# One-hots of four tiles: one comparison and one multiplication of 512 columns in place of four weighed comparisons of 128

## The chip, the cores and the metric

The kernel runs on one core of one Trainium2 chip. The metric is the device time of one launch in microseconds, the median of three runs. All data are fp32 unless said otherwise.

## The reference

A graph network of two layers over N = 6250 nodes with 96 features and E = 100000 edges, sorted by their target node `dst`, each with a source `src`, 32 edge features and an edge weight. Layer 0 computes for each edge a message and a gate from the source's row and the edge's features, sums the gated messages over `dst`, updates every node and normalizes it. Layer 1 is a weighted graph convolution on the new rows x.

```python
src, dst = edge_index
edge_input = concatenate([x[src], edge_attr], axis=-1)
messages = gelu(edge_input @ mW1 + mb1) @ mW2 + mb2
gates = sigmoid(gelu(edge_input @ gW1 + gb1) @ gW2 + gb2)
aggregated = segment_sum(messages * gates, dst, num_segments=N)
...
deg = segment_sum(ew, col, num_segments=N)
norm = dinv[row] * ew * dinv[col]
out = segment_sum((x @ W)[row] * norm[:, None], col, num_segments=N)
```

Each layer's output is added to its input and layer-normalized once more.

## The kernel before

Edges are taken in tiles of 128 (one edge per partition), 8 tiles to a group, 98 groups. Two passes go over the edges, one for each layer.

**Pass 1** is written out group by group for the five engines, which meet only in semaphores. For group g:

- POOL (GpSimd) gathers the 128 source rows of each tile from memory with one indirect DMA (`gathers`, L534), 8 in a group. There are 8 buffers `rows`, so POOL may run up to 8 groups ahead; it waits on `s_xt`, which PE raises when a buffer has been transposed. The addresses come from the SBUF tensor `idx`, one column for each gather.
- PE transposes the rows of the next group (`transposes`, L632) and multiplies by the first weights (L659, L662) into PSUM; ACT copies the transposed rows (L897) and applies gelu (L913).
- DVE multiplies by the gate's weights and sums (L1240, L1243); ACT squashes the result (L931); DVE makes the gate (L1216, L1218) and gates the messages (L1219).
- DVE makes one-hots of the target's place in a window of 72 nodes (`one_hot`, L1153), PE sums with them (L605), and DVE adds the window into `acc1` (L1170).
- Beside this the nodes whose edges are all done are updated block by block (`block1_sums`, `block1_rows`: L1312 to L1352 on DVE).

**Preparing pass 2 in pass 1.** For about half of the groups (`DENSE`), pass 2 doesn't gather. Pass 1 makes for each tile a small matrix "weight by source and target", as a product of two one-hot matrices: `low` says which of 128 places in its block the edge's source has, times the edge weight, and `place` says which cell (block of the source, target) it goes to. 96 batches of four tiles are made, one in each step from group 2 on. `tile_hots(n)` is DVE's part: it waits until PE has read the ring's half that it is about to write, and calls `hots`, which writes four matrices of 128 columns into `ring_low` (L1256) and one of 2000 columns into `ring_place` (`place_hots`, L1250). Then it raises `s_tile_hot`. PE multiplies the two (`two_cells`, L685, into ps_xt and ps_hid), ACT copies the cells (L953), and SP writes them to `b_table` in memory. `places_ps`, the row of numbers 0 to 249 with which the one-hots are compared, lies in PSUM; `src_low` (in the tensor `dst_i`), `weight` and `cell` lie in SBUF.

**Pass 2** loads `b_table` (SP), multiplies it by the scaled rows (L741), gathers rows for the remaining groups (L534 again, from `x1s_table`), and writes the output. The gathers of pass 2 need the table of new rows, which is whole only after pass 1.

The order of DVE's work in a step of pass 1 is: gate, window, one-hots, node block, L1240, drain, L1243, `tile_hots`. On DVE an instruction may start a little before the one ahead of it has ended; `drain` waits until that one has written.

Of the kernel before, what the change touches and what calls it, by code (L numbers as in the profile page):

```python
# [5 lines left out]
P = 128  # L6
# [29 lines left out]
DENSE = [g for first, n in RUNS for g in range(first, first + n)]  # L36
# [12 lines left out]
MADE = 4  # L49
# [50 lines left out]
def gnn_kernel(nc, t, out):  # L100
    fp32, i32, bf16 = mybir.dt.float32, mybir.dt.int32, mybir.dt.bfloat16
    ALU = mybir.AluOpType
# [9 lines left out]
    with ctx:  # L112
        def sb(name, shape, dt=fp32):
            return ctx.enter_context(nc.sbuf_tensor(name, shape, dt))

        def sem(name):
            return ctx.enter_context(nc.semaphore(name))
# [41 lines left out]
        weight = sb("weight", [P, NT])  # L159
# [25 lines left out]
        ring_low = shared[:, 0:CELLS_AT].rearrange("p (k c) -> p k c", k=RING)  # L185
        ring_place = shared[:, CELLS_AT:READY_AT].rearrange("p (k c) -> p k c", k=2 * RING)
# [21 lines left out]
        src_low = dst_i[:, :].bitcast(fp32)  # L208
# [37 lines left out]
        places_ps = ps_fix[:, 0:HW]  # L246
# [62 lines left out]
        s_tile_hot = sem("s_tile_hot")  # L309
# [28 lines left out]
        def wait(eng, s, count):  # L338

            if not isinstance(count, int) or count > 0:  # L340
                eng.wait_ge(s, count)
# [696 lines left out]
        def _(dve):  # L1038
# [84 lines left out]
            def column(ap):  # L1123
                return ap.rearrange("p (k o) -> p k o", o=1)
# [8 lines left out]
            for m, low_nodes in enumerate(tile_low_ps):  # L1133
                mine = slice(NT // 2 * m, NT // 2 * (m + 1))
# [87 lines left out]
            def step1(k, v, easy, b):  # L1222
                g, u = SLOTS * k + v, v % 2
                if u == 0 and not (isinstance(g, int) and g == 0):
                    gate1(g - 1, 1)
                if not (isinstance(g, int) and g < 2):
                    window1(g - 2, u, easy)

                one_hot(hot[u], dst_rel[:, ds(TG * g, TG)])
                nc.vector.tensor_tensor(vals[u][:, :, ND + 1:VC], column(weight[:, ds(TG * g, TG)]),  # L1230
                                        column(places_ps[:, 0:1]).to_broadcast([P, TG, 1]), ALU.add)
                if u == 1:
                    gate1(g - 1, 0)
                if b is not None:
                    pair1(b)
                if easy and g + 1 == CELL_AT:
                    tile_hots(0)

                dve.wait_ge(s_gelu, 2 * g + 2)
                nc.vector.tensor_tensor(prod[:, :, :], hid[u][:, :, ND:HC],  # L1240
                                        gw2_ps.rearrange("p (o c) -> p o c", o=1).to_broadcast([P, TG, ND]), ALU.mult)
                nc.vector.drain()
                nc.vector.tensor_reduce(logit[u][:, :], prod[:, :, :], AX, ALU.add).then_inc(s_logit, 1)  # L1243
                if easy and CELL_AT < g + 2 < NG:
                    tile_hots(g + 2 - CELL_AT)

            def place_hots(g, ks, place):
                shape = [P, 2 * len(ks), HW]
                cells = cell[:, TG * g + ks[0]:TG * g + ks[-1] + 1, :].rearrange("p k (h o) -> p (k h) o", o=1)
                return nc.vector.tensor_tensor(place, cells.to_broadcast(shape),  # L1250
                                               places_ps.rearrange("p (o w) -> p o w", o=1).to_broadcast(shape), ALU.is_equal)

            def hots(g, ks, low, place):
                t0 = TG * g
                for i, k in enumerate(ks):
                    nc.vector.tensor_scalar(low[:, i, :], places_ps[:, 0:P], src_low[:, t0 + k:t0 + k + 1],  # L1256
                                            weight[:, t0 + k:t0 + k + 1], ALU.is_equal, ALU.mult)
                return place_hots(g, ks, place)

            def early_hots(e, m):  # L1260
                ks = range(TG // 2 * m, TG // 2 * (m + 1))
# [15 lines left out]
            def tile_hots(n):  # L1277
                wait(dve, s_tile_cells, 2 * (n - 1))
                r = MADE * (n % 2)
                hots(DENSE[n // 2], range(r, r + MADE), ring_low[:, r:r + MADE, :], ring_place[:, 2 * r:2 * (r + MADE), :]).then_inc(s_tile_hot, 1)  # L1280

            def close1(easy=False):
                gate1(NG - 1, 1)
# [251 lines left out]
```

## Time and profile before

| | |
|---|---|
| median of 3 runs | 1505.38 us (1504.96 to 1505.86) |
| the profiled execution | 1507.1 us, of which the span from first to last instruction 1505.3 us |
| PE busy | 1397.7 us (93%) |
| DVE busy | 1087.5 us (72%) |
| ACT busy | 536.7 us (36%) |
| POOL busy | 1119.1 us (74%) |
| granted TensorE clock | 0.984 of full speed, mean |

Engines: PE is TensorE (PEld its weight loads), DVE VectorE, ACT ScalarE, POOL GpSimd, SP SyncE. Busy time counts compute instructions and POOL's indirect DMA instructions; waits and issues of the other queues are not in it. A share is of the span. Pass 1 fills about the first 1000 us. L with a number is a line of the kernel.

### The profile page before, as it was taken

How to read it: one execution, taken by the hardware profiler on the slowest of the kernel's cores; microseconds unless marked ns; L12 is line 12 of the kernel's file. 1: busy time of each engine (PE TensorE's matmuls, PEld its weight loads, DVE VectorE, ACT ScalarE, POOL GpSimd, SP SyncE). 2: the span in 40 equal slices, each digit the busy share in tenths (PEclk: the TensorE clock that was granted, in tenths of full speed). 3: DMA queues.
4: the chain of work that ended last, by engine and by line, in shares of the span. 5: the costliest groups of instructions: out<-in, count | busy, mean ns of one | idle time of the engine just before them, and what ended most of it. 6: DMA issues, size and time to landing. Idle time of an engine off the chain costs nothing.

```text
span 1505.3 us, 27016 instructions
## 1 busy us (share of the span) xinstructions
PE 1397.7 (93%) x9260; PEld 1156.5 (77%) x9261; DVE 1087.5 (72%) x2883; ACT 536.7 (36%) x835; POOL 1119.1 (74%) x1192
## 2 busy tenths in 40 slices
PE   3899999999999999999999999987999999999887
PEld 2677777777777777777777677767999999998887
DVE  7688899989999988888899888867434343334234
ACT  1355555555555555555555555540000000000000
POOL 7777777777777777777777777775777777777774
PEclk9899999999999999999999999988999999999999
DMA  3455555555565556555655565557567877777772
GB/s 100 135 151 151 176 169 168 154 173 165 168 174 180 155 152 187 155 156 162 187 168 156 153 183 168 153 182 261 204 209 280 289 264 276 263 266 262 261 239 64
DMA packets 137992, 283.06 MB, mean 188 GB/s; under 512 B 53235, under 2 KB 102387, under 8 KB 137852
## 3 DMA queue, kind: packets, MB, share of 16 engines
q1 hardware_dynamic: 88860, 208.35, 38.3%
q0 software_dynamic: 37760, 58.07, 17.5%
q10 hardware_dynamic: 11232, 14.85, 3.4%
q8 instruction: 77, 1.26, 0.3%
q14 instruction: 63, 0.52, 0.1%
HBM read 176.08 MB, written 105.09 MB: 187 GB/s over the span
## 4 chain that ended last, share of the span: by engine, by line
PE 72%; POOL 7%; DMA 5%; DVE 4%; issue 4%; ACT 3%; DVEq 2%; SPq 0%; ACTq 0%
PE ps_hid L662 15%; PE ps_hid L685 11%; PE ps_xt L685 10%; PE ps_xt L741 10%; PE ps_win L605 9%; POOL rows L534 7%; PE ps_xt L632 5%; DMA large<-b_table 4%; PE ps_hid L659 4%; PE ps_win L823 3%; ACT large L913 3%; PE ps_bt L702 1%; DVE shared L1250 1%; PE ps_bn L716 1%; PE ps_bn L795 1%
## 5 line engine op out<-in xcount | busy, mean ns | idle before, releaser
L534 POOL DMA_INDIRECT rows<-in_x_nat,idx x782 | 741.5, 948 | 238.4 <-issue 238.0
L534 POOL DMA_INDIRECT rows<-x1s_table,idx x360 | 339.7, 944 | 118.5 <-issue 109.1
L741 PE MATMUL ps_xt<-large,x_nat 128*96 128x160 f32 (+1 forms) x2548 | 350.9, 293 | 12.8 <-DMA large<-b_table 12.8
L741 PEld LDWEIGHTS ps_xt<-large,x_nat 128*96 128x96 f32 x2548 | 333.5, 163 | 16.2 <-DMA large<-b_table 9.4
L662 PE MATMUL ps_hid<-mats,large 128*128 128x192 f32 x1568 | 321.2, 328 | 0.0
L662 PEld LDWEIGHTS ps_hid<-mats,large 128*128 128x128 f32 x1568 | 268.3, 191 | 44.2 <-issue 31.6
L913 ACT ACTIVATE large<-ps_hid 128x768 f32<-128x768 f32 x196 | 158.9, 811 | 165.2 <-PE ps_hid L662 165.2
L1250 DVE TENSOR_TENSOR shared<-cell,ps_fix 128x2000 f32<-128x2000 f32 x96 | 213.7, 2226 | 0.0
L685 PE MATMUL ps_hid<-shared 128*128 128x500 f32 x384 | 184.0, 601 | 22.5 <-ACT large L913 22.5
L685 PE MATMUL ps_xt<-shared 128*128 128x500 f32 x384 | 179.8, 591 | 6.0 <-DVE shared L1250 6.0
L953 ACT ACTIVATE shared<-ps_hid 128x1000 f32<-128x1000 f32 x96 | 96.4, 1005 | 198.3 <-PE ps_hid L685 198.3
L605 PEld LDWEIGHTS ps_win<-hot,large 128*98 128x98 f32 x1568 | 144.9, 167 | 18.3 <-issue 15.3
L605 PE MATMUL ps_win<-hot,large 128*98 128x72 f32 x1568 | 152.4, 250 | 5.5 <-DVE acc L1170 3.6
L1009 ACT ACTIVATE shared<-ps_xt 96x160 f32<-96x160 f32 (+1 forms) x26 | 7.5, 289 | 404.5 <-PE ps_xt L741 404.5
L659 PE MATMUL ps_hid<-b_split,ones_b 128*128 128x384 bf16 x392 | 128.8, 329 | 5.7 <-DVE step L1115 4.0
L1256 DVE TENSOR_SCALAR shared<-ps_fix,dst_i,weight 128x128 f32<-128x128 f32 x384 | 130.4, 401 | 2.0 <-PE ps_hid L685 2.0
L953 ACT ACTIVATE shared<-ps_xt 128x1000 f32<-128x1000 f32 x96 | 96.4, 1004 | 87.5 <-PE ps_xt L685 78.9
L685 PEld LDWEIGHTS ps_xt<-shared 128*128 128x128 f32 x384 | 69.8, 192 | 73.3 <-issue 67.0
L685 PEld LDWEIGHTS ps_hid<-shared 128*128 128x128 f32 x384 | 65.3, 190 | 76.9 <-issue 44.0
L632 PE MATMUL ps_xt<-ident,rows 128*96 128x128 f32 x784 | 103.5, 276 | 12.3 <-DMA rows<-in_x_nat,idx 6.7
L897 ACT ACTIVATE large<-ps_xt 96x1024 f32<-96x1024 f32 x98 | 99.9, 1019 | 36.0 <-PE ps_xt L632 30.3
L1444 DVE TENSOR_TENSOR acc<-acc,ps_win 96x72 f32 x97 | 21.9, 226 | 121.2 <-PE ps_win L810 105.9
(177 smaller groups left out, 1471.6 us busy)
## 6 DMA issues: line engine op xcount, KB each, us to landing
b_table<-shared SPq DMA_DIRECT2D x192, 500.0 KB
large<-b_table SPq DMA_DIRECT2D x96, 1000.0 KB, 5.2
rows<-in_x_nat,idx POOLq DMA_INDIRECT x782
large<-in_edge_t ACTq DMA_DIRECT2D x96, 128.0 KB
rows<-x1s_table,idx POOLq DMA_INDIRECT x366, 2.9
large<-in_x_t SPq DMA_DIRECT2D x7, 336.0 KB
x_nat<-in_x_nat SPq DMA_DIRECT2D x7, 336.0 KB
out_nodes<-shared SPq DMA_DIRECT2D x46, 48.0 KB
```

The source lines that it names most:

```text
L534: nc.gpsimd.indirect_dma_start(out=rows[slot][:, k, :], out_offset=None, in_=table, in_offset=bass.IndirectOffsetOnAxis(ap=idx[:, TG * g + ...
L605: mm = nc.tensor.matmul(ps_win[0:rws, 0:W], lhs[:, k, :], hot[u][:, k, :], start=(k == 0), stop=(k == TG - 1))
L632: mm = nc.tensor.transpose(ps_xt[m // 4][0:ND, P * (m % 4):P * (m % 4 + 1)], rows[v][:, m, :], ident[:, :])
L659: nc.tensor.matmul(ps_hid[j][:, 0:2 * HC], ones_b[:, :], flat(b1_split[:, :, :]), start=True, stop=False)
L662: mm = nc.tensor.matmul(ps_hid[j][:, HC * q:HC * (q + 1)], feat[u][:, P * m:P * (m + 1)], w1[:, :], start=False, stop=(q == 1))
L685: mm = nc.tensor.matmul(ps_pair[pair][:, m, 0:CELLS], ring_low[:, r, :], flat(ring_place[:, 2 * r:2 * r + 2, :]), start=True, stop=True)
L741: mm = nc.tensor.matmul(raw_sums(q), x_nat[:, c, :], stored_cells(q, c), start=(c == 0), stop=(c == NB - 1))
L897: nc.scalar.activation(feat[u][0:ND, :].rearrange("p (m c) -> p m c", m=2), ps_pair[0][0:ND, :, :], ACT.Copy).then_inc(s_feat, 1)
L913: nc.scalar.activation(flat(hid[u][:, 4 * half:4 * half + 4, :]).rearrange("p (j c) -> p j c", j=2), ps_pair[1][:, :, 0:2 * HC], ACT.Gelu) ...
L953: nc.scalar.activation(ready_b[i % READY].rearrange("p (h m x) -> p m h x", h=2, m=2), ps_pair[pair][:, :, 0:CELLS].rearrange("p m (h x) - ...
L1250: return nc.vector.tensor_tensor(place, cells.to_broadcast(shape), places_ps.rearrange("p (o w) -> p o w", o=1).to_broadcast(shape), ALU.i ...
L1256: nc.vector.tensor_scalar(low[:, i, :], places_ps[:, 0:P], src_low[:, t0 + k:t0 + k + 1], weight[:, t0 + k:t0 + k + 1], ALU.is_equal, ALU. ...
```

## The change

In `hots` the four instructions that compared and weighed one tile each go. One comparison fills the 512 columns of the four tiles with ones and zeros. After `place_hots` and a drain, one multiplication weighs them in place. The semaphore is raised by this multiplication; before it was raised by `place_hots`. `early_hots`, which makes the like for four other groups, stays as it was.

```diff
             def hots(g, ks, low, place):
                 t0 = TG * g
-                for i, k in enumerate(ks):
-                    nc.vector.tensor_scalar(low[:, i, :], places_ps[:, 0:P], src_low[:, t0 + k:t0 + k + 1],
-                                            weight[:, t0 + k:t0 + k + 1], ALU.is_equal, ALU.mult)
-                return place_hots(g, ks, place)
+                mine = slice(t0 + ks[0], t0 + ks[-1] + 1)
+                wide = [P, len(ks), P]
+                nc.vector.tensor_tensor(low, column(src_low[:, mine]).to_broadcast(wide),
+                                        places_ps[:, 0:P].rearrange("p (o c) -> p o c", o=1).to_broadcast(wide), ALU.is_equal)
+                place_hots(g, ks, place)
+                nc.vector.drain()
+                nc.vector.tensor_tensor(low, low, column(weight[:, mine]).to_broadcast(wide), ALU.mult).then_inc(s_tile_hot, 1)
...
-                hots(DENSE[n // 2], range(r, r + MADE), ring_low[:, r:r + MADE, :], ring_place[:, 2 * r:2 * (r + MADE), :]).then_inc(s_tile_hot, 1)
+                hots(DENSE[n // 2], range(r, r + MADE), ring_low[:, r:r + MADE, :], ring_place[:, 2 * r:2 * (r + MADE), :])
```

## Rows read from the trace of the kernel before

**Rows 1.** The page, busy time of two engines: us, share of the span, instructions.

```profile
PE 1397.7 (93%) x9260; PEld 1156.5 (77%) x9261; DVE 1087.5 (72%) x2883; ACT 536.7 (36%) x835; POOL 1119.1 (74%) x1192
```

**Rows 2.** The view of line L534: duration ns min/median/max, first and last start; its waits.

```profile
L534 POOL DMA_INDIRECT rows<-in_x_nat,idx x782: 940/944/1802, 2.9 to 981.5; - x196
L534 POOL DMA_INDIRECT rows<-x1s_table,idx x360: 938/944/982, 1031.8 to 1480.0; - x180
...
  DMA x1s_table<-x_nat: 9.1, 1
```

**Rows 3.** Timeline, POOL and PE, groups 5, 49 and 95: start us, us, instruction.

```profile
64.18 0.94 POOL L534 DMA_INDIRECT rows<-in_x_nat,idx  x1 [0.30 <-issue]
...
72.49 1.04 PE L632 MATMUL ps_xt<-ident,rows 128*96 128x128 f32 x8
...
503.79 0.94 POOL L534 DMA_INDIRECT rows<-in_x_nat,idx  x1 [0.30 <-issue]
...
506.49 1.05 PE L632 MATMUL ps_xt<-ident,rows 128*96 128x128 f32 x8
...
964.03 0.94 POOL L534 DMA_INDIRECT rows<-in_x_nat,idx  x1 [0.30 <-issue]
...
966.84 1.04 PE L632 MATMUL ps_xt<-ident,rows 128*96 128x128 f32 x8
```

**Rows 4.** Groups of instructions by line, DVE, 0 to 1060 us: count, busy us, mean ns.

```profile
L1250 DVE TENSOR_TENSOR shared<-cell,ps_fix 128x2000 f32<-128x2000 f32 x96 | 213.7, 2226 | 0.0
L1256 DVE TENSOR_SCALAR shared<-ps_fix,dst_i,weight 128x128 f32<-128x128 f32 x384 | 130.4, 401 | 2.0 <-PE ps_hid L685 2.0
...
L1240 DVE TENSOR_TENSOR prod<-large,ps_fix 128x768 f32<-128x768 f32 x98 | 92.7, 946 | 1.1 <-ACT large L913 1.0
```

**Rows 5.** Timeline of one batch (all engines; DVE, POOL), and of the next one's end.

```profile
501.75 0.94 DVE L1219 TENSOR_TENSOR large<-large,ps_fix 128x768 f32<-128x768 f32 x1
...
502.61 0.95 DVE L1240 TENSOR_TENSOR prod<-large,ps_fix 128x768 f32<-128x768 f32 x1
...
503.63 0.95 DVE L1243 TENSOR_REDUCE logit<-prod 128x8 f32<-128x768 f32 x1
...
504.50 1.36 DVE L1256 TENSOR_SCALAR shared<-ps_fix,dst_i,weight 128x128 f32<-128x128 f32 x4
...
505.78 2.23 DVE L1250 TENSOR_TENSOR shared<-cell,ps_fix 128x2000 f32<-128x2000 f32 x1
...
507.54 0.95 POOL L534 DMA_INDIRECT rows<-in_x_nat,idx  x1 [0.30 <-issue]
...
518.42 2.23 DVE L1250 TENSOR_TENSOR shared<-cell,ps_fix 128x2000 f32<-128x2000 f32 x1
...
522.86 0.61 PE L685 MATMUL ps_xt<-shared 128*128 128x500 f32 x1
```

**Rows 6.** The view of line L1318: duration ns min/median/max, first and last start, forms.

```profile
L1318 DVE TENSOR_TENSOR x1b<-x_nat,once x24: 247/347/547, 97.4 to 1015.1; 128x192 f32<-128x192 f32 x22, 128x96 f32<-128x96 f32 x1, 128x384 f32<-128x384 f32 x1
```

**Rows 7.** Timeline: stretched gathers and what DVE runs when they start.

```profile
139.11 0.97 POOL L534 DMA_INDIRECT rows<-in_x_nat,idx  x1 [0.30 <-issue]
...
892.54 0.35 DVE L1318 TENSOR_TENSOR x1b<-x_nat,once 128x192 f32<-128x192 f32 x1
...
892.57 1.14 POOL L534 DMA_INDIRECT rows<-in_x_nat,idx  x1 [0.30 <-issue]
...
956.14 0.53 DVE L1352 SCALAR_TENSOR_TENSOR h<-h_g,root,x1b 128x96 f32<-128x96 f32 x2
...
956.45 1.03 POOL L534 DMA_INDIRECT rows<-in_x_nat,idx  x1 [0.30 <-issue]
...
1015.08 0.55 DVE L1318 TENSOR_TENSOR x1b<-x_nat,once 128x384 f32<-128x384 f32 x1
...
1015.22 1.22 POOL L519 DMA_INDIRECT rows<-x1s_early,idx_early  x1 [0.30 <-issue]
```

**Rows 8.** Who waited for whom: us in total, times, longest.

```profile
DVE ps_fix L1216 <- ACT squash L931: 52.9, 67, 6.8
```

## The prediction, made before the changed kernel ran

> **What bounds the kernel now.** I read the page's busy shares first. PE is busy for 93% of the span and DVE for 72% [rows 1], so at first sight the change works on an engine that has room, and whose time costs only what PE waits for. PE is then the engine to follow, but its share doesn't say what paces it. The gathers do, for a good part of pass 1. POOL issues 782 of them in pass 1, the first at 2.9 us and the last at 981.5 us, and each takes 0.944 us in the median [rows 2]. The same instruction in pass 2 goes 360 times from 1031.8 to 1480.0 us, so 448.2 / 359 = 1.248 us from one start to the next. In pass 1 it is (981.5 - 2.9) / 781 = 1.253 us. POOL has no pause in pass 1; its one long one (9.1 us, for the x1s_table) comes after it. A group needs 8 gathers, so POOL can't serve groups faster than one in 8 x 1.248 = 9.99 us.
>
> Next I set the transposes of a group (L632, PE) beside the start of its last gather [rows 3]. In group 5 they come 72.49 - 64.18 = 8.31 us after it, in group 49 506.49 - 503.79 = 2.70 us, in group 95 966.84 - 964.03 = 2.81 us. Between groups 5 and 49 PE takes (506.49 - 72.49) / 44 = 9.86 us a group, between 49 and 95 (966.84 - 506.49) / 46 = 10.01 us. So PE is the faster one at first and eats its stock of gathered rows, and from about 500 us on, when the distance has come down to some 2.7 us (the time in which a gather lands), it goes at POOL's pace. Whatever delays POOL in pass 1, early or late, therefore arrives in full at the end of pass 1; what DVE saves there buys nothing while PE waits for rows.
>
> **The change part by part.** It is made 96 times, once for each batch of four tiles.
>
> *Removed*: four comparisons of 128 columns, L1256. One lasts 401 ns [rows 4], but they overlap: from the first of four (504.50) to the start of the next instruction, L1250 (505.78), it is 1.28 us [rows 5], or 320 ns each.
>
> *Added, comparison of 512 columns.* It reads PSUM and one SBUF column, like L1240 (768 columns, 946 ns) and L1250 (2000 columns, 2226 ns) [rows 4]. The slope is 1280 / 1232 = 1.04 ns a column, so 512 columns last 946 - 256 x 1.04 = 680 ns. L1219 (768 columns, 501.75) is followed by L1240 at 502.61, 0.86 us later, though it lasts 0.94: 0.08 less than its length [rows 5]. The comparison then takes 0.60 us of DVE.
>
> *Added, drain and multiplication.* After L1240 a drain stands and L1243 starts 1.02 us later [rows 5], 0.07 after its end. The multiplication reads two SBUF tensors, and the nearest row is L1318: 247, 347 and 547 ns for 96, 192 and 384 columns [rows 6], so 547 + 128 x 1.04 = 680 ns for 512. Waiting for place_hots costs 0.08 (the overlap lost) + 0.07, and the multiplication 0.60 if the next instruction overlaps it again. DVE has 0.60 + 0.15 + 0.60 = 1.35 us in place of 1.28, 0.07 more in each batch, 6.7 us in all.
>
> *What hides these 6.7 us*: DVE waits 52.9 us for ACT's squash in 67 places [rows 8], and PE takes the one-hots late: L1250 started at 518.42 ends at 520.65, and PE begins the cells of that batch (L685, ps_xt) at 522.86 [rows 5], 2.2 us later, against 0.07 us. If the cover were gone they would cost 6.7 us at most. I take 0. In the very first batch nothing covers the 0.07, but PE has a stock of rows to eat afterwards.
>
> *Memory ports.* This is the term that decides. Eleven of the gathers between 60 us and the end of pass 1 are over 965 ns long, the first at 139.11 and the last at 956.45 [rows 7]; I looked at what DVE does when each starts, and in all eleven it is in an instruction whose tensors all lie in SBUF. The plainest is L1318, the nearest row to the new multiplication: it runs 892.54 to 892.89, the gather starts at 892.57 and lasts 1.14 instead of 0.94. The wide form runs 1015.08 to 1015.63, the gather starts at 1015.22 and lasts 1.22. Distance from the gather's start to the end of the DVE instruction: 0.32 and 0.41; stretch of the gather: 0.20 and 0.28. So the gather waits until about 0.125 us before that end. The next gather starts later by as much, since the pause of 0.30 stays. Instructions with a PSUM input do nothing of the kind: L1250 runs over a gather start at 507.54, which stays at 0.95 [rows 5]. The four removed instructions read PSUM too, so they give nothing back.
>
> The new multiplication (680 ns, two SBUF inputs, in place of none) blocks gathers that start in its first 0.680 - 0.125 = 0.555 us. Gather starts are 1.248 us apart, so 0.555 / 1.248 = 0.44 of the multiplications meet one, and it waits 0.28 us on average: 0.123 us for each. Times 96: 11.8 us. In place at 504.50 the multiplication would run about 504.50 + 0.60 + 2.23 + 0.07 = 507.40 to 508.08, and the gather at 507.54 [rows 5] would wait 0.41. Bounds: nothing, if this instruction doesn't block; 96 x 0.555 = 53 us, if each meets a gather at its very start. I take the mean over phases, because the distance between batches changes and is no multiple of 1.248 (12.64 us between the two L1250 shown [rows 5], 10.01 a group on the mean), which spreads them.
>
> The Trainium skill bears on this. "SBUF — State Buffer", section "Who interferes with whom", says that a VectorE instruction with two SBUF inputs contends with a GpSimd instruction that reads SBUF, and that one with at most one SBUF input does not; the rows above agree. The same section says that tensor_tensor was not seen to stall a DMA issued from GpSimd; the stretched gathers beside L1318 say that it does here, by 0.20 and 0.28 us. "VectorE: DVE Perf Modes", section on the TRN2 errata, speaks for the change: latency is paid between instructions, and tiles of 512 or more spread it. By its formula (N + 151) / 0.96 GHz two of 512 columns are an estimated 1.38 us, above the 1.28 us that the four take here, so even by that page DVE gains nothing.
>
> **The sum.** Profiled execution 1507.1 us (span 1505.3) + 11.8 (gathers) + 0 (DVE) = 1518.9. That execution is 1.7 us above the median of the runs, 1505.4, so the forecast is 1517.2. Pass 2 begins later by the delay of pass 1 and keeps its length; nothing in it is touched.
>
> **Rivals.**
> - *Phases lock on the bad side.* Once PE goes at POOL's pace, each batch keeps a set distance from a gather, and a delay shifts both. With half of full blocking on all 96 it is 27 us, 1532 us. For it: the lock exists in half of pass 1. Against: distances that change from batch to batch, and each delay moves the next phase.
> - *The port doesn't matter for this instruction* (not slower). L1318 is the only two-tensor instruction of any width here, met 22 times in pass 1, and most of its meetings leave no mark, because the gather started before it or late in it. If the stretch had another cause, only the hidden 0.07 is left: 1505.4 us, and at most 1512 with the cover gone. The skill's sentence on tensor_tensor and DMAs from GpSimd would give this too.
> - *DVE gets faster and PE follows.* It decides if the drain and the overlap cost nothing: 2 x 0.60 = 1.20 against 1.28. But POOL's pace holds: 782 gathers at 1.248 us need 976 us, and they take 979, so at most 3 us are to be had, 1502 us.
>
> **How the numbers follow.** A measurement here tells 0.2%, about 3 us, from no change. Mean phases: 0.74, and its own range is 1510 to 1523 (0.05 to 0.18 us each, as phases fall). Locked on the bad side: 0.09. No contention: 0.13. Faster: 0.04. Slower 0.83, same 0.13, faster 0.04. The range must leave out no more than 2 in 10, so it reaches down to the case of no contention: 1505 to 1524.
>
> **What would show it.** Gathers of pass 1 (L534): median still 0.944, mean up from 948 to near 1070 ns, with some 40 of them stretched by 0.1 to 0.55 us, each beside the new multiplication; the last one near 993 us instead of 981.5. Comparison and multiplication near 680 ns. The distance of transposes to last gather reaches 2.7 us near group 27 instead of 49. The wait for squash shrinks a little. I am wrong if the last gather stays at 981.5 us, or if it moves by over 20 us.

## The result, and the profile after

The changed kernel takes 1519.53 us (median of four runs, 1518.72 to 1522.53), the kernel before 1505.62: a ratio of 1.0093, with an interval of 1.0078 to 1.0107. The forecast was 11.8 us more; it is 13.9. The two profiled executions are 11.6 us apart (spans of 1516.9 and 1505.3 us).

The place to look first is POOL, on which not a line was changed. Groups of instructions by line, of the kernel after (count, busy us, mean ns, idle before):

```profile
L534 POOL DMA_INDIRECT rows<-in_x_nat,idx x782 | 756.7, 968 | 238.4 <-issue 238.0 <-DMA idx<-in_src_t 0.4
```

The page of before has 741.5 us and a mean of 948 ns for these 782 gathers. They take 15.2 us more, and the pauses between them are the same 238.4. The view of that line shows that it is not all of them:

```profile
L534 POOL DMA_INDIRECT rows<-in_x_nat,idx x782: 940/944/1807, 2.9 to 996.7; - x196
L534 POOL DMA_INDIRECT rows<-x1s_table,idx x360: 940/944/953, 1043.7 to 1491.9; - x180
...
  DMA x1s_table<-x_nat: 5.9, 1
```

The median stays at 944 ns. The last gather of pass 1 starts at 996.7 instead of 981.5 [rows 2], 15.2 us later, and those of pass 2 are untouched: 448.2 us from first to last, as before. DVE, by groups:

```profile
L1250 DVE TENSOR_TENSOR shared<-cell,ps_fix 128x2000 f32<-128x2000 f32 x96 | 214.1, 2230 | 0.0
...
L1261 DVE TENSOR_TENSOR shared<-shared,weight 128x512 f32<-128x512 f32 x96 | 66.5, 693 | 7.5 <-issue 0.4
L1257 DVE TENSOR_TENSOR shared<-dst_i,ps_fix 128x512 f32<-128x512 f32 x96 | 65.1, 678 | 2.1 <-PE ps_hid L685 2.1
```

L1257 is the comparison (680 ns forecast), L1261 the multiplication (680). What the second one does to POOL is seen in the timeline, twice in the first half and then in two batches in a row:

```profile
302.80 0.69 DVE L1261 TENSOR_TENSOR shared<-shared,weight 128x512 f32<-128x512 f32 x1
303.20 1.11 POOL L534 DMA_INDIRECT rows<-in_x_nat,idx  x1 [0.30 <-issue]
...
310.81 0.69 DVE L1261 TENSOR_TENSOR shared<-shared,weight 128x512 f32<-128x512 f32 x1
...
310.85 1.47 POOL L534 DMA_INDIRECT rows<-in_x_nat,idx  x1 [0.30 <-issue]
...
569.53 0.69 DVE L1261 TENSOR_TENSOR shared<-shared,weight 128x512 f32<-128x512 f32 x1
...
570.00 1.04 POOL L534 DMA_INDIRECT rows<-in_x_nat,idx  x1 [0.30 <-issue]
...
577.27 0.69 DVE L1261 TENSOR_TENSOR shared<-shared,weight 128x512 f32<-128x512 f32 x1
...
577.59 1.20 POOL L534 DMA_INDIRECT rows<-in_x_nat,idx  x1 [0.30 <-issue]
```

Read the second pair: the multiplication ends at 311.50, the gather starts 0.65 before that and is 0.53 longer than 0.94. In the first pair it is 0.29 and 0.17. The difference is 0.12 both times, what the forecast had from L1318 [rows 7]. Laid over all 96 multiplications, 69 have a gather start between their own start and 0.125 us before their end. The rule (the gather waits until 0.125 us before the end) gives 15.9 us for these 69, the trace shows 15.7, and no single one is off by more than 7 ns. None of the 69 starts less than 0.04 us after the multiplication; what happens nearer to its start is told at the end.

PE then waits for the rows. Who waited for whom, of after (us in total, times, longest):

```profile
PE ps_xt L632 <- issue: 18.3, 12, 3.4
```

In the kernel before the same line of the waits has 5.4 us in 5 places. The view names no releaser here ("issue"), so that these are waits for rows is read from the distance between a group's last gather and its transposes. It is already down to 2.7 us in group 29 (forecast: near 27), where before it took until group 49 [rows 3]:

```profile
307.11 0.94 POOL L534 DMA_INDIRECT rows<-in_x_nat,idx  x1 [0.30 <-issue]
...
309.83 0.60 PE L632 MATMUL ps_xt<-ident,rows 128*96 128x128 f32 x4
...
978.97 0.95 POOL L534 DMA_INDIRECT rows<-in_x_nat,idx  x1 [0.30 <-issue]
...
981.89 1.04 PE L632 MATMUL ps_xt<-ident,rows 128*96 128x128 f32 x8
```

The lower two rows are group 95: 2.92 us, and it comes 15.05 us later than before. So the delay does arrive in full at the end of pass 1. The first gather of pass 2 is late by 11.9 us (1043.7 against 1031.8), 3 less, which this one execution gained in handing over the table of new rows. In the later profile of the same kernel (e10, below) the last gather of pass 1 is 14.2 us late and the first of pass 2 13.2. From the last gather of pass 1 to the first of pass 2 it is 47.0 us here and 49.0 to 50.3 in before, e1, e4, e5, e8, e9 and e10, so most of the 3 us is this execution's own and not shown to be something that the change gives back.

### The profile page after: what moved, and what is told of

The parts are those of the page before. It is cut to its first block, busy times and chain, and to the rows that moved or that the text cites. A ratio compares the mean times of both kernels' runs of the same rounds, so it can differ in the third digit from the quotient of the medians.

```text
span 1516.9 us, 26920 instructions
## 1 busy us (share of the span) xinstructions
PE 1397.0 (92%) x9260; PEld 1156.3 (76%) x9261; DVE 1090.4 (72%) x2691; ACT 536.6 (35%) x835; POOL 1134.2 (75%) x1192
## 4 chain that ended last, share of the span: by engine, by line
PE 66%; POOL 14%; issue 7%; DVE 4%; ACT 3%; DMA 1%; DVEq 1%; SPq 0%; ACTq 0%
PE ps_hid L662 15%; POOL rows L534 14%; PE ps_hid L685 11%; PE ps_xt L685 10%; PE ps_win L605 9%; PE ps_xt L741 6%; PE ps_xt L632 5%; PE ps_hid L659 4%; ACT large L913 3%; PE ps_win L823 2%; DMA large<-b_table 1%; DVE shared L1250 1%; PE ps_bt L702 1%; PE ps_bn L716 1%; PE ps_hid L834 1%
## 5 line engine op out<-in xcount | busy, mean ns | idle before, releaser
L534 POOL DMA_INDIRECT rows<-in_x_nat,idx x782 | 756.7, 968 | 238.4 <-issue 238.0
L534 POOL DMA_INDIRECT rows<-x1s_table,idx x360 | 339.7, 944 | 115.3 <-issue 109.1
L741 PE MATMUL ps_xt<-large,x_nat 128*96 128x160 f32 (+1 forms) x2548 | 350.0, 293 | 14.7 <-DMA large<-b_table 14.7
L1250 DVE TENSOR_TENSOR shared<-cell,ps_fix 128x2000 f32<-128x2000 f32 x96 | 214.1, 2230 | 0.0
L605 PEld LDWEIGHTS ps_win<-hot,large 128*98 128x98 f32 x1568 | 145.6, 168 | 17.9 <-issue 15.2
L632 PEld LDWEIGHTS ps_xt<-ident,rows 128*96 128x96 f32 x784 | 88.9, 128 | 33.0 <-issue 21.9
```

The lines of the kernel that those rows point to most:

```text
L534: nc.gpsimd.indirect_dma_start(out=rows[slot][:, k, :], out_offset=None, in_=table, in_offset=bass.IndirectOffsetOnAxis(ap=idx[:, TG * g + ...
L605: mm = nc.tensor.matmul(ps_win[0:rws, 0:W], lhs[:, k, :], hot[u][:, k, :], start=(k == 0), stop=(k == TG - 1))
L632: mm = nc.tensor.transpose(ps_xt[m // 4][0:ND, P * (m % 4):P * (m % 4 + 1)], rows[v][:, m, :], ident[:, :])
L741: mm = nc.tensor.matmul(raw_sums(q), x_nat[:, c, :], stored_cells(q, c), start=(c == 0), stop=(c == NB - 1))
```

## The experiments

The theory: the multiplication's second SBUF input blocks the gathers, and gathers pace pass 1. The rivals: DVE's work (0.07 us more in each batch), or the one-hots that are announced later. Every kernel was timed beside the kernel before on its own chip, and each ratio is to that one.

### e1: the same multiplication, its weights read from PSUM

```diff
                 wide = [P, len(ks), P]
+                by = ps_fix[:, HW + ND + 2 * TG:HW + ND + 2 * TG + len(ks)]
+                nc.vector.tensor_copy(by, weight[:, mine])
...
-                nc.vector.tensor_tensor(low, low, column(weight[:, mine]).to_broadcast(wide), ALU.mult).then_inc(s_tile_hot, 1)
+                nc.vector.tensor_tensor(low, low, column(by).to_broadcast(wide), ALU.mult).then_inc(s_tile_hot, 1)
```

> The changed kernel, but the four weights of a batch are first copied into PSUM (128 x 4, one small DVE copy more), and the multiplication reads them there: one SBUF input instead of two, all else the same, the output too. Theory (the second SBUF input blocks the gathers): no gather is stretched beside the multiplication, the last gather of pass 1 comes at 981 to 983 us instead of 996.7, and the time is 1505 to 1508 us. Rival (DVE's longer work, or the one-hots coming later): DVE works 0.1 to 0.2 us more in each batch than in the changed kernel, so 1519 us or more.

Measured: 1507.89 us against 1506.89, ratio 1.0009 (0.9997 to 1.0021): the loss is gone. The groups of DVE and POOL:

```profile
L1263 DVE TENSOR_TENSOR shared<-shared,ps_fix 128x512 f32<-128x512 f32 x96 | 66.1, 689 | 7.5 <-issue 0.4
...
L1258 DVE COPY ps_fix<-weight 128x4 f32<-128x4 f32 x96 | 14.9, 155 | 2.1 <-PE ps_hid L685 2.1
```

```profile
L534 POOL DMA_INDIRECT rows<-in_x_nat,idx x782 | 741.3, 948 | 238.4 <-issue 238.0 <-DMA idx<-in_src_t 0.4
```

The multiplication is as long as in the changed kernel (689 against 693 ns), 46 gathers start in the part of it that would block, and none is stretched. One from the timeline:

```profile
511.33 0.69 DVE L1263 TENSOR_TENSOR shared<-shared,ps_fix 128x512 f32<-128x512 f32 x1
511.56 0.94 POOL L534 DMA_INDIRECT rows<-in_x_nat,idx  x1 [0.30 <-issue]
```

By the rule it would have waited 0.34 us, had the multiplication had two SBUF inputs. DVE does more here than in the changed kernel (the copy, 155 ns long, puts the start of L1250 back by 0.06 us), and the one-hots come later still, so both rivals fall.

### e2 and e3: the kernel before with one more multiplication, by ones from SBUF or from PSUM

```diff
-                return place_hots(g, ks, place)
+                place_hots(g, ks, place)
+                nc.vector.drain()
+                wide = [P, len(ks), P]
+                return nc.vector.tensor_tensor(low, low, column(ones[:, 0:len(ks)]).to_broadcast(wide), ALU.mult)
```

e3 has `column(places_ps[:, 1:2])` in place of `column(ones[:, 0:len(ks)])`.

> The kernel before, with its four weighed comparisons, and behind place_hots a drain and one more multiplication of the 512 columns by ones from SBUF; the output stays the same. Theory (port): about as many gathers are stretched as in the changed kernel, the last one of pass 1 comes 12 to 19 us later than before, 1516 to 1524 us. DVE has 0.75 us more work in each batch, 72 us in all, more than its wait for the squash (52.9 us), so some of the extra may be DVE's; the next run is the one to set beside it.

> The same as the run with the extra multiplication by ones from SBUF, but the one comes from PSUM (a column of places_ps that holds 1), so that the extra instruction has the same length and one SBUF input. Theory (port): no gather is stretched by it, and it is 8 us or more faster than its twin; if DVE's time is hidden it stands at 1505 to 1508 us. Rival (DVE's time): both twins take the same, 1515 us or more.

Measured: 1542.91 us (ratio 1.0246, 1.0233 to 1.0259) and 1541.34 (1.0232, 1.0215 to 1.0248). Both expectations missed: the twins are not 8 us apart, and both are some 35 us slower. The rival's forecast for the pair (DVE's time, both alike, 1515 us or more) is what came. Their waits for the squash and their gathers, e2 first and then e3:

```profile
DVE ps_fix L1216 <- ACT squash L931: 14.2, 7, 6.3
```

```profile
L534 POOL DMA_INDIRECT rows<-in_x_nat,idx x782 | 746.5, 955 | 238.4 <-issue 237.7 <-DMA idx<-in_src_t 0.4 <-PE ps_xt L632 0.3
```

```profile
DVE ps_fix L1216 <- ACT squash L931: 14.1, 7, 5.7
```

```profile
L534 POOL DMA_INDIRECT rows<-in_x_nat,idx x782 | 741.5, 948 | 238.4 <-issue 237.8 <-PE ps_xt L632 0.6
```

0.75 us more in each batch is 72 us of DVE, an estimate, and 34 to 36 of them show. The wait for the squash falls by 38.7 us, from 52.9: DVE used up about 37 us of room, and PE then fell behind POOL (in group 95 the transposes come 29.6 and 35.4 us after the last gather, not 2.8). The last gather of pass 1 is 5 us later in e2 than in e3 (986.5 against 981.5), and pass 2 doesn't begin later for it (1064.7 against 1065.5): POOL has slack there. So the pair measured DVE's room, not what the stretches cost. It does say that the gathers are stretched in the one and not in the other: 26 start in the extra multiplication of e2 ahead of its last 0.125 us, and all but one (shown at the end) wait as the rule says, 5.6 us in all; of the 37 that start so in that of e3 none does.

### e4: the comparison alone

```diff
-                place_hots(g, ks, place)
-                nc.vector.drain()
-                nc.vector.tensor_tensor(low, low, column(weight[:, mine]).to_broadcast(wide), ALU.mult).then_inc(s_tile_hot, 1)
+                place_hots(g, ks, place).then_inc(s_tile_hot, 1)
```

> The changed kernel without the multiplication and the drain: the one-hots stay unweighted, so the weights are left out of the sums of the dense groups. DVE works 1.28 - 0.60 = 0.68 us less in each batch than in the kernel before, 65 us in all, and nothing is stretched. Theory (POOL's gathers pace pass 1): 1503 to 1507 us, the time of the kernel before, although DVE has 65 us less to do. Rival (DVE's time counts): 1495 us or less.

Measured: 1507.98 us, ratio 1.0008 (0.9998 to 1.0019). By the estimate DVE has 65 us less to do than in the kernel before, and not one of them is gained. They lie for the most part in its waits for the squash, which were 52.9 us in 67 places [rows 8]:

```profile
DVE ps_fix L1216 <- ACT squash L931: 113.0, 77, 6.3
```

### e5: the multiplication in four of 128 columns

```diff
-                nc.vector.tensor_tensor(low, low, column(weight[:, mine]).to_broadcast(wide), ALU.mult).then_inc(s_tile_hot, 1)
+                for i, k in enumerate(ks):
+                    last = nc.vector.tensor_tensor(low[:, i:i + 1, :], low[:, i:i + 1, :],
+                                                   column(weight[:, t0 + k:t0 + k + 1]).to_broadcast([P, 1, P]), ALU.mult)
+                last.then_inc(s_tile_hot, 1)
```

> The changed kernel with the multiplication cut in four of 128 columns, each with two SBUF inputs as before; the same output. By the rows of L1318 and of the changed kernel one of 128 columns lasts about 281 ns and the next starts 195 ns later, so DVE works some 0.2 us more in each batch. Theory (an instruction blocks only the gathers that start between its start and 0.125 us before its end, and only until then): stretches of at most 0.16 us, gathers that start between two of them are free, 3 to 8 us in all, 1508 to 1514 us. Rival (a run of such instructions blocks as one, 0.86 us long): stretches of up to 0.7 us, 1525 us or more.

Measured: 1512.54 us beside 1509.58 for the kernel before on that chip, ratio 1.0013 (1.0000 to 1.0027), so some 2 us by the ratio and 3 by the medians: a seventh to a fifth of the changed kernel's loss, for the same columns from the same two SBUF tensors, and with more DVE time. 63 gathers start within one of the 96 runs of four and before its last 0.125 us; 20 of them are not stretched at all and no other by more than 0.13 us; in all it is 3.0 us. This one starts when the first of the four is nearly over and just before the second begins:

```profile
52.76 0.93 DVE L1262 TENSOR_TENSOR shared<-shared,weight 128x128 f32<-128x128 f32 x4
52.96 0.95 POOL L534 DMA_INDIRECT rows<-in_x_nat,idx  x1 [0.30 <-issue]
```

A gather waits for the one instruction that it met, not for the next. By the rule, and with gathers that start at any distance alike, the cost of a blocking instruction goes with the square of its length less 0.125 us: a longer one is met more often, and each meeting waits longer. Only these two lengths were run.

### e6 and e7: both kernels with a gather less in each group

```diff
-                for k in range(TG - (REST if last else 0)):
+                for k in range(min(TG - (REST if last else 0), TG - 1 if rows_sem is s_rows and g >= SLOTS else TG)):
...
-                pe.wait_ge(s_rows[v], group_rows(k, v))
+                last = isinstance(k, int) and SLOTS * k + v == NG - 1
+                pe.wait_ge(s_rows[v], 16 * ((TG - 1) * k + TG - (1 if last else 0)))
```

> The kernel before with 7 instead of 8 gathers in each group of pass 1 from group 8 on (the eighth tile keeps old rows, so part of the gathered data is left out): POOL has slack in pass 1. Theory (POOL paces pass 1 from about 500 us on): PE goes at its own 9.86 us a group to the end, pass 1 is some 7 us shorter, 1497 to 1501 us. If PE or DVE is the bound already: 1505 us.

> The changed kernel with the same 7 gathers in each group from group 8 on, to be set beside the kernel before with 7. Theory (the port's delays cost only because POOL paces pass 1): gathers are stretched as in the changed kernel, 8 to 16 us in sum, but the time is that of its twin within 3 us. Rival (the change costs by another way than the gathers, such as the later one-hots): it stays 10 us or more above its twin.

Measured: 1500.65 us (before, with 7) and 1501.27 (after, with 7), beside 1509.58. Groups of POOL's instructions, e6 first:

```profile
L534 POOL DMA_INDIRECT rows<-in_x_nat,idx x693 | 658.7, 951 | 248.0 <-issue 200.6 <-PE ps_xt L633 47.1 <-DMA idx<-in_src_t 0.3
```

```profile
L534 POOL DMA_INDIRECT rows<-in_x_nat,idx x693 | 667.7, 963 | 240.4 <-issue 201.8 <-PE ps_xt L633 38.3 <-DMA idx<-in_src_t 0.3
```

In e7 the gathers take 9.0 us longer, and POOL's wait for PE to free a buffer is 8.8 us shorter: the stretches are still there (56 meetings, 10.8 us; the other gathers are 3 ns shorter than in e6) and are paid out of slack. The change costs 0.6 us where POOL has slack, which is within the spread of these runs, and 13.9 where it has none. And e6 itself is 9 us (ratio 0.9942, 0.9922 to 0.9961) faster than the kernel before. PE takes 9.865 us a group between groups 5 and 49, as before (9.864), and 9.865 again between 49 and 95, where it took 10.01: with POOL's work cut, PE keeps its own pace to the end.

### e8: the comparison with two SBUF inputs as well

```diff
+            nc.vector.tensor_copy(ones[:, :], places_ps[:, 0:P])
...
-                                        places_ps[:, 0:P].rearrange("p (o c) -> p o c", o=1).to_broadcast(wide), ALU.is_equal)
+                                        ones[:, :].rearrange("p (o c) -> p o c", o=1).to_broadcast(wide), ALU.is_equal)
```

`ones` is free at that point and now holds 0 to 127 in each row.

> The changed kernel with the numbers 0 to 127 copied once into SBUF, and the comparison of 512 columns reading them there: the comparison too has two SBUF inputs now, the same length, the same output. Theory (port): twice as many chances to block a gather, so 5 to 17 us more than the changed kernel, 1524 to 1537 us, and gathers stretched beside both lines. Rival (what costs is the place or the drain of the multiplication): as the changed kernel, 1519 us.

Measured: 1533.52 us beside 1509.58, ratio 1.0153 (1.0130 to 1.0175), 23.9 us. Groups of DVE and POOL:

```profile
L1262 DVE TENSOR_TENSOR shared<-shared,weight 128x512 f32<-128x512 f32 x96 | 66.5, 693 | 7.2
L1258 DVE TENSOR_TENSOR shared<-dst_i,ones 128x512 f32<-128x512 f32 x96 | 65.6, 683 | 1.7 <-PE ps_hid L685 1.7
```

```profile
L534 POOL DMA_INDIRECT rows<-in_x_nat,idx x782 | 770.8, 986 | 238.5 <-issue 238.1 <-DMA idx<-in_src_t 0.3
```

The comparison is nearly as long as in the changed kernel (683 against 678 ns), and now it holds gathers up too: 23 that start in it are stretched by 5.3 us in all, counted from this profile's median of 947 ns, and 79 in the multiplication, by 21.0. The second source adds to the first, though not evenly.

### e9 and e10: the multiplication ahead of place_hots, and the changed kernel once more

```diff
-                place_hots(g, ks, place)
                 nc.vector.drain()
-                nc.vector.tensor_tensor(low, low, column(weight[:, mine]).to_broadcast(wide), ALU.mult).then_inc(s_tile_hot, 1)
+                nc.vector.tensor_tensor(low, low, column(weight[:, mine]).to_broadcast(wide), ALU.mult)
+                place_hots(g, ks, place).then_inc(s_tile_hot, 1)
```

> The changed kernel with drain and multiplication ahead of place_hots instead of behind it, so that place_hots raises the semaphore as before; the output and DVE's work per batch are the same. The multiplication runs 2.2 us earlier in each batch, at another distance from the gathers. Theory (port): it costs again, by the mean over phases 12 us, with 5 to 18 us as the phases fall, and each stretch still ends 0.125 us before the multiplication's end: 1511 to 1524 us. Rival (the late semaphore or the wait for place_hots costs): the time of the kernel before.

> The changed kernel as it is, beside the kernel before on this chip, for a tighter ratio and to set the run with the multiplication moved beside it. Every theory expects the first result again, 12 to 16 us above the kernel before.

Measured on one chip: 1521.80 us moved (ratio 1.0106, 1.0085 to 1.0126) and 1519.56 unmoved (1.0094, 1.0076 to 1.0112), beside 1506.61. The groups, e9 first:

```profile
L534 POOL DMA_INDIRECT rows<-in_x_nat,idx x782 | 753.7, 964 | 238.5 <-issue 237.8 <-DMA idx<-in_src_t 0.4 <-PE ps_xt L632 0.3
```

```profile
L534 POOL DMA_INDIRECT rows<-in_x_nat,idx x782 | 755.7, 966 | 238.4 <-issue 238.0 <-DMA idx<-in_src_t 0.4
```

Neither the place nor the late semaphore matters: the loss moves along with the instruction. At the other distance 52 gathers are held up instead of 65, and the stretches sum to 12.5 us instead of 14.7. The time of e9 isn't lower for it; 2 us are within what these runs spread.

## Why the prediction was right, point by point

- **What bounds the kernel** held. From about 500 us on the gathers pace pass 1: e4 takes an estimated 65 us of work from DVE and gains nothing, e6 takes a gather in eight from POOL and gains 9 us.
- **DVE's sum** held nearly: comparison 678 ns and multiplication 693 (680 each). That its 6.7 us are hidden was right: e1, with more of DVE's work still, stands level with the kernel before. But e2 and e3 show where the edge is: about 37 us of room in all, less than the 52.9 us of waits [rows 8] on which I leaned. 14 us of these waits stayed even there.
- **The port** (a DVE instruction with two tensors in SBUF holds up a gather that starts in it) held in its kind, by e1, e7, e8 and e9, and in the amount for each meeting: "until about 0.125 us before that end" is right within 7 ns in 69 cases. What the prediction said of L1318, that most of its meetings leave no mark, undersold its own evidence: in the kernel before five gathers start in it ahead of its last 0.125 us, and all five are stretched as the rule says, by 14 to 195 ns. Its other test, "an instruction whose tensors all lie in SBUF", is too wide. L1243 reads and writes SBUF alone and runs from 503.63 to 504.58 [rows 5]; the gather of 503.79 starts in it and keeps its 0.94 us [rows 3]. So it is with all 69 gathers that start in L1243 ahead of its last 0.125 us in the kernel before, and with all 78 in the changed one: none is longer by more than 3 ns. L1243 has one input.
- **The mean over phases** is the term that was too small. Forecast: 0.44 of the multiplications meet a gather and it waits 0.28 us, 0.123 us for each. Measured: 0.72 and 0.23 us, 0.164 us for each, 15.7 in all against 11.8. That the time came within 2.1 us of the forecast is partly luck, for the number of meetings was not under control: it is 46 in e1, 54 in e9, 65 in e10 and 79 in e8, each for the one multiplication. In part the rival of locked phases is seen: of the 40 stretched gathers from 490 us on, 12 last about 1.04 us and 16 about 1.20, 570.00 and 577.59 above being such a pair. Why the lock falls on distances that meet so often was not tried, except that e9 met fewer.
- **Two signs to look for** were wrong. A mean gather of "near 1070 ns" was a slip: 11.8 us over 782 gathers are 15 ns, so 963 (968 came). And DVE's wait for the squash didn't shrink: 53.8 us against 52.9. Where the gathers aren't the pace it did: 35.8 us in e7 against 46.2 in e6; and in e1, where they aren't stretched, it is 34.6. So PE's waits for rows seem to have made DVE wait too.
- **The page's two rules.** That two SBUF inputs contend with GpSimd's reads (the Trainium skill, "SBUF — State Buffer", "Who interferes with whom") is borne out by e1 against the changed kernel. The same section's remark that tensor_tensor doesn't stall such a DMA is not: 15.7 us here. That many small tiles pay a latency each ("VectorE: DVE Perf Modes" of the Trainium skill, section on the TRN2 errata) fits e5, whose four multiplications take 0.90 us instead of 0.69. Yet they were cheaper for the whole, because they let POOL in.

No version here that does the whole work beats the kernel before. Less work on DVE buys nothing in pass 1 (e4), and without the second SBUF input the change costs nothing either (e1): both stand level with it.

## What to carry to other kernels

Before widening or fusing VectorE instructions, look at where their tensors lie and whether GpSimd is issuing gathers meanwhile: here one that reads two tensors from SBUF held up a gather until it was nearly over, and the same one with an input in PSUM didn't. Two such costs belong side by side in a sum: the time on the engine that runs the instruction, and the delay of the other engine, which counts only if that engine sets the pace. An engine that is 74% busy can be the pace; to see it, set its last delivery beside the consumer's start, group by group.

## What was not expected of the hardware

- The delay is very exact: 69 meetings followed one rule within 7 ns, and a gather that started late in one short blocking instruction and ahead of the next went through (e5).
- When both start nearly together it can go the other way. In e2 one starts 0.04 us after the extra multiplication, keeps its 0.94 us, and the multiplication lasts 0.76 us instead of 0.69:

```profile
115.76 0.76 DVE L1261 TENSOR_TENSOR shared<-shared,ones 128x512 f32<-128x512 f32 x1
115.80 0.94 POOL L534 DMA_INDIRECT rows<-in_x_nat,idx  x1 [0.30 <-issue]
```

  In e5, e8 and e9 ten gathers that start within 0.02 us after a blocking instruction go through, and the instruction is longer. The edge isn't sharp: in e5 a gather that starts 0.03 us after one is held up.
- Once a gather has run for 0.06 us, a multiplication that starts beside it doesn't stretch it (76 cases in the changed kernel, at most 3 ns).
- Two inputs are not the whole rule. L1331 of the kernel before, a TENSOR_SCALAR that reads one tensor and a column of numbers, all in SBUF, also stretches the gathers that start in it, six of seven by 12 to 37 ns, within 7 ns of what the 0.125 us rule says. Why it does and L1243 doesn't, no run here shows.
- The gather's own length is not quite fixed: its median is 944 ns in most profiles and 947 in those of e5, e6 and e8, and beside these the kernel before took 1509.58 us, against 1505.62 to 1506.89 elsewhere. 1142 gathers (782 + 360) times 3 ns would be 3.4 us. But e7, from the same chip, has 944, so whether this is the cause stays open.
